# Graph attention on one Trainium2 core: the first two edge operations of the first block go from VectorE to GpSimd

## The reference

```python
h = jnp.maximum(_layernorm(x, axis=-1), 0.0)
Wh = h @ W                                   # 8192 x 64
a1, a2 = (a[:F_OUT, 0], a[F_OUT:, 0])
e = (Wh @ a1)[:, None] + (Wh @ a2)[None, :]  # 8192 x 8192
e = jax.nn.leaky_relu(e, negative_slope=ALPHA)
scores = jnp.where(adj > 0, e, jnp.float32(NEG_INF))
attention = jax.nn.softmax(scores, axis=1)
out = x + jax.nn.elu(attention @ Wh)
```

## Time and profile before

| | us |
|---|---|
| median of 3 runs | 683.38 (683.11 to 683.46) |
| the profiled execution's own time | 682.71 |
| its span in the trace | 680.8 |
| busy: TensorE / VectorE / ScalarE | 632.8 / 616.9 / 630.5 |
| busy: GpSimd | 60.2 |
| data moved by DMA | 275.16 MB, 404 GB/s over the span |

### The profile page before, as it was taken

The page is one execution under the profiler, slowest core; times in us unless marked ns, Lnnn a source line. Parts: engine busy times, 40 slices in busy tenths (PEclk is TensorE's granted clock), DMA queues, the critical chain, the costliest instruction groups (busy, mean ns, idle before and its releaser), DMA issues.

```text
span 680.8 us, 23844 instructions
## 1 busy us (share of the span) xinstructions
PE 632.8 (93%) x10422; PEld 620.1 (91%) x10422; DVE 616.9 (91%) x625; ACT 630.5 (93%) x366; POOL 60.2 (9%) x51
## 2 busy tenths in 40 slices
PE   4769999999998999999999999989898998989895
PEld 4648899999998999999999999989898998989895
DVE  6999899999989899889999999898989989898993
ACT  5998899999999998999999999989898998989981
POOL 5000101011010101011010201010010101001020
PEclk9969999999999999999999999999999999999999
DMA  9997899999999999999999999999999999999970
GB/s 320 426 426 286 328 420 410 422 427 427 428 424 430 428 425 425 429 428 425 427 425 429 428 425 428 426 427 426 427 427 426 427 427 428 425 427 428 424 301 19
DMA packets 24841, 275.16 MB, mean 404 GB/s; under 512 B 3088, under 2 KB 7440, under 8 KB 8432
## 3 DMA queue, kind: packets, MB, share of 16 engines
q1 hardware_dynamic: 22864, 270.67, 94.5%
q0 software_dynamic: 1488, 4.07, 1.6%
q10 hardware_dynamic: 464, 0.07, 0.1%
HBM read 272.70 MB, written 2.10 MB: 404 GB/s over the span
## 4 chain that ended last, share of the span: by engine, by line
DMA 32%; DVE 24%; ACT 20%; PE 14%; issue 10%; DVEq 1%; SPq 0%; ACTq 0%
DMA adj_ring<-in_adj 31%; DVE code L675 15%; ACT work L514 14%; PE psum L916 5%; PE psum L914 5%; ACT work L522 3%; DVE work L688 3%; PE psum L896 3%; DVE code L682 1%; PE psum L954 1%; DMA work<-in_x 1%; ACT trow L497 1%; DVE last_steps L706 1%; DVE last_steps L710 1%; DVE last_steps L699 1%
## 5 line engine op out<-in xcount | busy, mean ns | idle before, releaser
L916 PE MATMUL psum<-V,work 128*128 128x130 f16 x4096 | 492.1, 221 | 0.0
L914 PE MATMUL psum<-V,work 128*128 128x130 f16 x4096 | 491.7, 219 | 0.4 <-DVE work L688 0.4
L514 ACT ACTIVATE work<-trow,Wh 128x4096 int8<-128x4096 f32 x128 | 477.0, 3727 | 1.6 <-DVE code L682 1.6
L914 PEld LDWEIGHTS psum<-V,work 128*128 128x128 fp8e4 x4096 | 400.9, 98 | 0.5 <-issue 0.5
L916 PEld LDWEIGHTS psum<-V,work 128*128 128x128 fp8e4 x4096 | 398.0, 97 | 0.0
L675 DVE TENSOR_SCALAR code<-adj_ring 128x4096 uint8<-128x4096 int32 x128 | 293.0, 2290 | 26.4 <-DMA adj_ring<-in_adj 25.2
L682 DVE SCALAR_TENSOR_TENSOR code<-work,code 128x1024 int32<-128x1024 int32 x128 | 156.5, 1223 | 9.9 <-ACT work L514 7.5
L896 PE MATMUL psum<-identb,code 128*128 128x128 bf16 x2048 | 136.8, 221 | 24.2 <-DVE code L682 20.9
L522 ACT COPY work<-psum 128x1024 int32<-128x1024 int32 x128 | 129.9, 1015 | 26.2 <-PE psum L896 26.2
L896 PEld LDWEIGHTS psum<-identb,code 128*128 128x128 bf16 x2048 | 120.0, 98 | 29.9 <-DVE code L682 21.3
L688 DVE TENSOR_SCALAR work<-work 128x1024 int32<-128x1024 int32 x128 | 88.0, 687 | 3.3 <-ACT work L522 3.2
(11 more groups left out here) (76 smaller groups left out, 150.7 us busy)
## 6 DMA issues: line engine op xcount, KB each, us to landing
adj_ring<-in_adj SPq DMA_DIRECT2D x128, 2048.0 KB, 16.5
work<-in_x SPq DMA_DIRECT2D x4, 512.0 KB, 6.1
last_steps<-in_x POOLq DMA_DIRECT2D x16, 128.0 KB, 6.8
out_y<-last_steps POOLq DMA_DIRECT2D x15, 128.0 KB, 7.8
out_y<-last_steps SPq DMA_DIRECT2D x1, 128.0 KB, 1.9
W<-in_L_gnn_W ACTq DMA_DIRECT2D x2, 16.0 KB, 5.1
Wx<-in_L_gnn_W ACTq DMA_DIRECT2D x2, 16.0 KB, 5.5
a_sb<-in_L_gnn_a ACTq DMA_DIRECT2D x1, 0.5 KB, 4.0
```

What stands on the lines that cost most here:

```text
L514: nc.scalar.activation(sign[:, k % 2].bitcast(I8), trow[:, h * UW:(h + 1) * UW], ACT.Sign, bias=(Wh[:, B, 0:1] if isinstance(B, int) else ...
L914: nc.tensor.matmul(sums_of[:, 0:FP], up8[:, j // 2, j % 2], V[:, jb, 0:FP], start=h == 0 and j == 0, stop=False, skip_group_check=True)
L916: last = nc.tensor.matmul(sums_of[:, FP:2 * FP], down8[:, j // 2, j % 2], V[:, jb, FP:2 * FP], start=False, stop=h == 1 and j == HB - 1, s ...
```

## The change

The edge operations of units 0 and 1 of block 0 are issued on GpSimd instead of VectorE, after the four mean subtractions. The operation and its operands are the same. A new semaphore `s_edge0` counts the two. `load_when_free` for loads 4 and 5, and `codes` for units 0 and 1, wait for it instead of for `s_edge`. VectorE adds 2 to `s_edge` ahead of its queue, so that all later counts stay as they are. The rest of VectorE's queue keeps its order.

```diff
+        s_edge0 = sem("edge_codes_of_a_first_unit_written")
...
+        EARLY = 2
...
                 def load_when_free(i, k, c):
-                    sp.wait_ge(s_edge, (i * BU + k) * UT + c - RT + 1)
+                    if isinstance(i, int) and i == 0 and k - KE < EARLY:
+                        sp.wait_ge(s_edge0, k - KE + 1)
+                    else:
+                        sp.wait_ge(s_edge, (i * BU + k) * UT + c - RT + 1)
                     load(i, k, c)
...
+                for k in range(EARLY):
+                    pool.wait_ge(s_adj[k], 16)
+                    nc.gpsimd.tensor_scalar(code[:, k, :], adj_ring[:, k, :], 0.0, float(EDGE), ALU.is_gt, ALU.mult)\
+                        .then_inc(s_edge0, 1)
...
                 def codes(i, k):
-                    dve.wait_ge(s_edge, (i * BU + k + 1) * UT)
+                    if isinstance(i, int) and i == 0 and k < EARLY:
+                        dve.wait_ge(s_edge0, k + 1)
+                    else:
+                        dve.wait_ge(s_edge, (i * BU + k + 1) * UT)
...
+                dve.sem_inc(s_edge, EARLY)
                 row_sums(0)
...
                 copy_Wh(0)
-                edges(0, 0)
                 copy_Wh(1)
                 variance(3)
-                edges(0, 1)
                 copy_Wh(2)
                 edges(0, 2)
```

## The result

The changed kernel takes 696.63 us (median of 4, 695.53 to 697.66) beside 683.25 for the kernel before: ratio 1.0208, 95% interval 1.0196 to 1.0221. The two medians are 13.4 us apart; the ratio stands for 14.2 us, and 13.4 is the lower end of its interval. The profiled execution took 695.53 with a span of 693.6, 12.8 us over the span before.

A forecast was written before the change was run, and what follows sets the result against it. The stream of 2 MB loads, 5.0 us each, was taken as the bound. Of 4.4 us removed from VectorE 1.3 was usable; a 4.9 us stall made net +3.6, less 1.2 slack +2.4: 685.8 us, range 682.8 to 692.0.

The forecast's parts named there:

- The price of GpSimd's operation: Two edge operations on GpSimd behind the mean subtractions: 7.0 us each, running 16.1 to 23.1 and 23.1 to 30.1.
- T: Length of one GpSimd edge operation of 4096 elements: taken as 7.0 us, with bounds 2.8 and 9.0.
- The stop of VectorE: VectorE's edges(0, 2), ready at 25.2, waits for GpSimd's second operation and starts at 30.1 instead of 26.5: +3.6 us.
- s = 2T - 10.4: Delay s of edges(0, 2) on VectorE, from T, the length of one GpSimd operation; +3.6 us at T = 7.0.
- The candidate that it did have: copy_Wh on VectorE, if stopped too: copy_Wh(0) waits from 16.7 to 23.1 or 30.1; end +7.8 us, 691.2.
- GpSimd slower, or more of VectorE stopped: Rival for the opening: T = 9.0 gives 689.8, copy_Wh stopped too gives 691.2; chance 0.16.
- VectorE's 4.4 us: Removing edges(0, 0) and edges(0, 1) takes 4.4 us off VectorE's queue; 1.3 usable, 3.1 become idle time.
- Load 4 and load 5 stay hidden: SyncE's loads issued at 23.2 (needed by 28.6) and 30.2 (needed by 33.6); load 5 late with T above about 8.7.
- The slack of 1.2 us: ScalarE's slack at its Exp, 34.05: ScalarE and TensorE move by s - 1.2, edges(0, 8) and load 12 by +2.4 us.
- its own sign of being wrong: The prediction is wrong if TensorE's clock changes the length of its sum over all nodes by over 1 us.
- The way to the end: edges(0, 8) and load 12 move by s - 1.2, +2.4 us; the stream is full from load 12 on.
- ScalarE's wait for TensorE at 61.23: A 3.01 us wait for transposes, read as part of the chain ScalarE, TensorE, ScalarE behind the gap ahead of load 12.

The follow-up runs named there:

- the bench: The kernel before, with eleven operations on GpSimd alone added behind its end, one after the other; the edge operation of 4096 elements took 14.02 us.
- left_out: The changed kernel without GpSimd's two edge operations; GpSimd clears those codes and signals when the loads have landed: ratio 0.9994 to the kernel before.
- cast_only: The changed kernel with a plain tensor_copy on GpSimd in place of each edge operation: ratio 1.0000 to the kernel before.
- order: The kernel before, with edges(0, 6) moved ahead of codes(0, 4) and edges(0, 8) ahead of low_parts(3) in VectorE's queue: ratio 1.0002.
- early_transpose: The kernel before, with TensorE's transposes of unit (0, 3) moved ahead of the first products: 680.66 us, ratio 0.9976.

## Why the prediction was wrong, and where it was right

**The price of GpSimd's operation: this failed.** "I take T = 7.0, since that is the only row of GpSimd on a long tile, and keep 2.8 and 9.0." It was 14.0. The row was of a tensor_tensor, and for a tensor_tensor of 4096 elements the bench gives 7.01. A tensor_scalar with two steps takes twice that. The upper bound was no bound: it came from one short affine_select of 128 elements, again another kind of operation. The range inherited this and ended at 692.0. The estimate of 3.4 us, worked out from what the Trainium skill says of one-input operations (GPSIMD Engine Reference, Engine selection), holds for the copy, 3.60, and is off by four for this operation; the measurement decides.

**The stop of VectorE: right.** `edges(0, 2)` was ready at 25.2 as forecast and stood until GpSimd was done. What was missed is that it is let in between GpSimd's two operations when the first is long: s = 2T - 10.4 holds only while the second has begun by 25.2. The second then stopped the 3x4 step, which the prediction did not have among its candidates. With T = 14 the formula would have said +16.4 at the end, and it was 12.8 in the trace. The candidate that it did have, `copy_Wh`, was not stopped: beside GpSimd's first operation the pair took 1.34 us at 16.56, as before. So the rival "GpSimd slower, or more of VectorE stopped", which had a chance of 0.16, was right in kind and wrong in both of its prices, 689.8 and 691.2.

**VectorE's 4.4 us are worth nothing: right.** left_out and cast_only, both within 0.2% of the kernel before.

**Load 4 and load 5 stay hidden: wrong through T.** They were issued at 30.1 and 46.1, not 23.2 and 30.2; the prediction's own limit of 8.7 us for load 5 was passed by far.

**The slack of 1.2 us: right, and kept to the end with some luck.** `edges(0, 6)` is 14.1 us late, ScalarE's Exp 12.9, and the end 12.8. In between the lower clock of TensorE made ScalarE 14.0 us late, and the shorter sum over all nodes gave 1.07 us back. The prediction had no term for either; its own sign of being wrong, the sum changed by over 1 us, was just met, and as the two cancel it isn't what made the forecast miss. VectorE's idle time of 1.77 us at `low_parts(3)` shrank to 0.67, by 1.1.

**The way to the end: right in size, in part wrong in mechanism.** "`edges(0, 8)` and load 12 move by s - 1.2 ..., and from load 12 on the stream is full." Load 12 and ScalarE move together in the change, so the sum came out by luck. When order moved loads 10 and 12 alone, nothing followed; when early_transpose moved TensorE's step and ScalarE with it, and left load 10 in place, the end did. The stream is what sets the pace only from about 200 us on; up to there, as far as these runs show, ScalarE and TensorE set it. That ScalarE's wait for TensorE at 61.23 belonged to the chain was read correctly.

**What was not forecast:** that the stop alone gives the full loss and the wait of `codes(0, 1)` alone most of it (two thirds by my estimate), and so the rival "more of VectorE stopped" could not be told by its price from "slower GpSimd".

## What to carry to other kernels

Before work goes to another engine, find a row of that engine for the same kind of instruction, with the same number of arithmetic steps; one of another kind can be off by a factor of two to four in the same tile size. Work given to GpSimd can make VectorE wait in two ways, for its result and while it runs; price both, since here each alone was worth two thirds of the loss or more. And when a resource seems to have gaps near the start, move it alone before believing that it sets the end: here the loads had 9 us of gaps, closing some of them gave nothing, and one step of TensorE moved ahead by some 4 us gave 0.24%.

## What the runs showed of the hardware that was not expected

On GpSimd, 4096 elements in each partition took 3.60 us as a copy with conversion, 7.01 as a float32 tensor_tensor, 10.55 as a tensor_scalar with one step and 14.02 with two, the tensor_scalar within 0.04 us of this in every pair of types that was run. A tensor_scalar of 3x4 elements on VectorE, which takes 0.22 us otherwise, took 11.13 beside it. And VectorE is let in between two GpSimd operations that are issued back to back, even though the second had no wait of its own: 16.00 us instead of 14.04 for it. A scalar_tensor_tensor with two SBUF inputs waited too, 5.40 us instead of 1.2, but ended 1.5 us before GpSimd's operation.
